# GpSimd rounds the context of the cross-attention, and ScalarE writes one more mask

## What is computed

```python
K = split(jnp.einsum('bsd,ed->bse', key, wk))
V = split(jnp.einsum('bsd,ed->bse', value, wv))
scores = jnp.einsum('bhqd,bhkd->bhqk', Q, K) / np.sqrt(hd)
scores = jnp.where(mask[:, None, :, :] == 1, jnp.float32(-1000000000.0), scores)
attn = jax.nn.softmax(scores, axis=-1)
out = jnp.einsum('bhqk,bhkd->bhqd', attn, V)
```

## Time and profile before

| | |
|---|---|
| median of three runs | 1336.21 us (1335.66 to 1337.94) |
| the profiled execution | 1324.22 us, of which the span takes 1322.4 |
| mean granted TensorE clock | 0.967 of full speed |
| busy: TensorE matmuls, VectorE, ScalarE, GpSimd | 1221.1, 899.4, 761.3, 498.6 us |
| the steps of the attention | about 498 to 1054 us of the span |

### The profile page before, as it was taken

How to read it: one execution, slowest core, us unless ns; L and a number is a source line. 1 busy time by engine, 2 the same in 40 slices (tenths; PEclk the granted TensorE clock), 3 DMA queues, 4 the chain that set the end, 5 groups by cost and what they waited for, 6 DMA issues and landing times.

```text
span 1322.4 us, 34415 instructions
## 1 busy us (share of the span) xinstructions
PE 1221.1 (92%) x10866; PEld 1107.4 (84%) x10866; DVE 899.4 (68%) x2932; ACT 761.3 (58%) x1780; POOL 498.6 (38%) x709
## 2 busy tenths in 40 slices
PE   5899999999997788999999999999999988999984
PEld 4788889899897677889999999899998777888884
DVE  4684664856746456788788888888887575555548
ACT  3444344333442226788888888888888854555530
POOL 2332240422412323344444444444444541333335
PEclk9999999999998898999999999999999898999997
DMA  8499700000000235566666665556665143333358
GB/s 206 106 232 239 176 0 0 0 0 0 0 0 23 57 76 140 141 142 153 153 149 154 152 151 148 145 147 150 152 157 148 52 136 93 101 106 98 106 141 249
DMA packets 131263, 151.39 MB, mean 114 GB/s; under 512 B 41107, under 2 KB 111108, under 8 KB 131156
## 3 DMA queue, kind: packets, MB, share of 16 engines
q1 hardware_dynamic: 124436, 134.55, 42.1%
q0 software_dynamic: 6160, 15.69, 3.5%
q10 hardware_dynamic: 576, 0.07, 0.0%
HBM read 79.27 MB, written 45.82 MB: 95 GB/s over the span
## 4 chain that ended last, share of the span: by engine, by line
PE 50%; DVE 4%; issue 2%; ACT 2%; DMA 2%; POOL 1%; SPq 1%; DVEq 0%; POOLq 0%; ACTq 0%
PE psum L875 9%; PE psum L1124 7%; PE psum L1161 6%; PE psum L1147 6%; PE psum L1296 6%; PE psum L1316 3%; PE psum L1093 2%; PE psum L1142 2%; PE psum L1189 2%; PE psum L1175 1%; DVE x_res L2333 1%; PE psum L1208 1%; PE psum L1287 1%; PE psum L1304 1%; DVE x_res L2327 1%
## 5 line engine op out<-in xcount | busy, mean ns | idle before, releaser
L2196 DVE CUSTOM_DVE_ANT_0 junk<-psum,biasq 112x375 f32<-112x375 f32 x512 | 267.5, 542 | 93.2 <-issue 60.1
L1653 ACT ACTIVATE pr<-psum 125x448 f32<-125x448 f32 x384 | 204.1, 540 | 37.5 <-PE psum L1147 35.8
L1147 PE MATMUL psum<-qst,kst 97*125 97x224 f32 x768 | 194.4, 319 | 5.4 <-ACT psum L1662 5.2
L1124 PE MATMUL psum<-kst,qst 96*112 96x376 f32 x512 | 170.1, 357 | 3.6 <-DVE smax L2196 3.2
L1147 PEld LDWEIGHTS psum<-qst,kst 97*125 97x125 f32 x768 | 139.2, 192 | 19.6 <-ACT psum L1662 13.2
L1662 ACT ACTIVATE psum<-flagk 125x448 f32<-125x448 bf16 x256 | 140.4, 549 | 6.7
L717 POOL TENSOR_TENSOR rs<-rs,neg_half 112x1 f32<-112x1 f32 x32 | 18.2, 569 | 244.3 <-DVE rs L2109 244.3
L841 POOL DMA_INDIRECT routed_y<-yb,yrow x61 | 58.7, 962 | 123.9 <-ACT yb L1843 119.7
L1124 PEld LDWEIGHTS psum<-kst,qst 96*112 96x112 f32 x512 | 89.8, 180 | 15.0 <-issue 5.8
L1161 PE MATMUL psum<-pr,vaug 125*32 125x112 f32 x3072 | 96.3, 267 | 0.0
L759 POOL DMA_INDIRECT routed_h<-h,slot x64 | 74.7, 1166 | 32.3 <-POOL h L748 14.8
(11 more groups left out here) (320 smaller groups left out, 3529.5 us busy)
## 6 DMA issues: line engine op xcount, KB each, us to landing
kst<-khi SPq DMA_DIRECT2D x64, 376.0 KB, 4.9
routed_h<-in_route_pad SPq DMA_DIRECT2D x6, 3640.0 KB
kst<-klo SPq DMA_DIRECT2D x32, 376.0 KB, 6.1
ctxT<-in_ctxT SPq DMA_DIRECT2D x32, 375.0 KB, 3.5
hblk<-routed_h SPq DMA_DIRECT2D x61, 130.0 KB, 2.1
qst<-qhi SPq DMA_DIRECT2D x128, 56.0 KB, 2.5
stage<-in_e SPq DMA_DIRECT2D x21, 256.0 KB, 3.1
maskq<-in_mask SPq DMA_DIRECT2D x32, 164.1 KB
```

Of the source, the lines that this page charges most:

```text
L1124: pe.matmul(bank[max_bank(n, par, hd)][0:T, 0:S2E], head(qst[par][0:ROWS], hd), pair(kst[par][0:ROWS], hd // 2), start=True, stop=True).th ...
L1147: mm = pe.matmul(bank[q % 2][0:KP, cols(i, 2 * T)], pair(kst[par], n)[:, cols(q // HPB, KP)], both(qst[par], n), start=False, stop=True, s ...
L1653: nc.scalar.activation(pr[q % PROBS][:].rearrange("k i q -> k (i q)"), bank[q % 2][0:KP, 0:GT], ACT.Exp, scale=1.0 / HD ** 0.5).then_inc(s ...
L2196: nc.vector.tensor_tensor_reduce(out=junk[:, hd % 2, :], in0=bank[max_bank(n, par, hd)][0:T, 0:S2], in1=biasq[:, par, :], scale=1.0, scala ...
```

## The change

ScalarE no longer rounds the context from row 3 on. GpSimd does it with a `tensor_copy`, for row b + 3 in step b, right behind its second power and ahead of `decide`. Slot 11 joins the table of written slots: ScalarE writes its mask behind the exponential of slot 9, and TensorE's mask matmul of slot 11 falls away.

```diff
-WRITTEN = (2, 3, 4, 6, 7, 8, 9, 10)
+WRITTEN = (2, 3, 4, 6, 7, 8, 9, 10, 11)
@@ GpSimd
+            def high_context(t, par):
+                f = t * RB + par
+                wait_apart(pool, s2["ctx_in"], 16 * (f + 1))
+                wait_apart(pool, s2["v_ps"], f)
+                nc.gpsimd.tensor_copy(chi[:, :, 0:S2], ctxT[:]).then_inc(s2["c_hi"], 1)
@@ GpSimd, step
                 if power:
                     rsqrt(*ahead(t, par, 3))
+                if context:
+                    high_context(*ahead(t, par, 3))
                 if early >= 2:
                     decide(*ahead(t, par, -2))
@@ ScalarE, step
-                    if q == 0 and following >= 2 and not first:
-                        high_context(*far)
...
-                    if q + 2 in WRITTEN and q < 8:
+                    if q + 2 in WRITTEN and q != 8:
                         write_mask(t, par, q + 2)
```

More of the change, by code:

```diff
@@ L769, in low_shared, with step @@
                 nc.gpsimd.tensor_tensor(h3lo[g % 2][:], raw, h3hi[g % 2][:].bitcast(F32), op=ALU.subtract).then_inc(s["ht_lo"], 1)
-            def step(t, par, masks=True, power=True):
+            def step(t, par, masks=True, power=True, context=True):
                 early = t * RB + par if isinstance(t, int) else 2 * RB
@@ L814, in _ @@
             for par in range(RB):
-                step(ROUNDS, par, power=ROUNDS * RB + par + 3 < B)
-            step(ROUNDS + 1, 0, masks=False, power=False)
+                step(ROUNDS, par, power=ROUNDS * RB + par + 3 < B, context=ROUNDS * RB + par + 3 < B)
+            step(ROUNDS + 1, 0, masks=False, power=False, context=False)
             scatter(*ahead(ROUNDS + 1, 1, -4))
```

## The result

Beside the same runs of the kernel before, the change takes 1344.3 us (median of 6) where that one takes 1336.3: ratio 1.0056, 95% interval 1.0043 to 1.0070. That is slower by about 8.0 us, inside the range given and 5.8 us above the forecast.

The account below looks back on a forecast made before the run. TensorE and ScalarE were taken to run in step, so the removed matmul becomes a wait. Terms +1.2, +0.8 and +0.3 sum to +2.3 us on the median 1336.2: 1338.5 us, range 1333 to 1345.5.

Parts of the forecast that it names:

- the same: Whole kernel: time change within 0.2% (2.7 us), what a measurement can tell from no change; chance 0.51.
- term 2: Slot 11 on TensorE: ScalarE's mask comes too late, next load 0.04 us later in 29 steps, +1.2 us.
- term 6: Between steps 1 and 2: cast ahead of GpSimd's three subtractions delays VectorE's scaling L2114 and TensorE by 0.80 us, +0.8 us.
- Terms 1 and 2: Slot 11: TensorE's mask matmul of 0.18 us a step goes, replaced by a wait for ScalarE's mask; +1.2 us.
- Matmul won: Rival, slot 11: the mask matmul's 0.18 us is saved in every step, 5.4 us in all, 1332 us; chance 0.13.
- Terms 3 to 5: Cast leaves ScalarE, takes 0.80 us on GpSimd, blocks VectorE's scaling; TensorE's transposes still met with 0.27 us spare; cost 0.
- Term 7: GpSimd's `decide`, scatter and masks move 0.8 us back; their readers come a step or more later: 0.
- Term 8: Step 30, no keys or values to make: ScalarE's mask delays slot 11's exponential, +0.3 us.
- The base: Starting time: profiled execution 1324.2 us, 12 us below the median; same difference put on the median, 1336.2 to 1338.5 us.

Follow-up runs that it names:

- e12: The change, unedited, third comparison against the kernel before: 1325.7 us beside 1322.6, ratio 1.0026 (1.0017 to 1.0034).
- e11: The kernel before, unedited, profiled a third time: 1322.2 us beside 1322.6, ratio 1.0000 (0.9990 to 1.0011).
- e7: Kernel before plus only GpSimd's cast, with the scatter moved behind the masks: 1321.8 us beside 1321.7, ratio 0.9998 (0.9986 to 1.0011).
- e9: The change, unedited, compared again with the kernel before: 1341.2 us beside 1336.5, ratio 1.0036 (1.0023 to 1.0049).
- e3: The whole change plus GpSimd's scatter moved behind the masks, against the kernel before: 1332.5 us beside 1335.2, ratio 0.9975 (0.9963 to 0.9986).
- e10: The change with the scatter behind the masks, e3 unedited, against the kernel before: 1332.5 us beside 1336.5, ratio 0.9972 (0.9959 to 0.9984).
- e5: Kernel before with only GpSimd's scatter moved behind the masks: 1323.1 us beside 1321.7, ratio 1.0009 (1.0000 to 1.0019).

## Why the prediction was right and wrong

The direction of the sum and the range held; the forecast of "the same" (0.51) did not. That 1344.3 us lies in the range is in part luck: its upper end stood for a cast of up to 1.3 us, and the cast took 0.80. The forecast itself reached to 1341 us. On the lower level, where its rows came from, the sum of +2.3 us met +3.4, with two errors against each other: term 2 was 2.5 us short, term 6 1.5 us too high.

- **Terms 1 and 2** (the mask matmul traded for a wait; 96 mask matmuls are left of 128): right in mechanism and to 0.01 us at slot 11's load. The step that failed is "with 0.22 us for the two scores the next load comes at 814.89": true in one step of three, 0.18 us short in the others, where four sequencer entries that used to be worked off ahead come only after the wait. 0.04 us a step was 0.16, +1.2 us was +3.7 (e12 against e11). "Matmul won" (0.13) never showed.
- **Terms 3 to 5** (cast off ScalarE, 0.80 us on GpSimd, L2120 blocked until 0.15 us after it, transposes met): right, 800 ns, 1.41 us, and no cost in e7. The cast starts at 826.36 and the next instruction at 827.14, so the spacing of starts gives 0.78 us; the 1.02 us that the Trainium skill's rule of spacings (Perfetto Trace Analysis, section "GPSIMD Engine Instruction") gave from the small cast was too long, because 0.22 of that cast's 0.60 us was the next instruction's wait for it.
- **Term 6**: wrong in sign. I let the cast lengthen the block of L2114; it came in between, after L2120 was through, and the block moved to a scaling that no transpose waits for. The first five steps together came out at about -0.7 us, where the term had +0.8; what else moved in them is not taken apart.
- **Term 7** (choice of experts and scatter 0.8 us later, "0"): right on the lower level. On the upper it is the step that failed: I asked only who reads the results of these instructions, not what their issue does to others. The change loses 8.0 and 4.7 us there and 3.4 on the lower level; 1.3 to 4.6 us more than its own cost go with the held signals, and moving the scatter, nothing else, takes 8.7 us away beside e9, and by the two ratios about 10.8 between e3 and the change's first comparison. Shown is that the scatter's place matters; how the cast and the mask divide the rest is not.
- **Term 8**: +0.07 us in the last three steps, where the term had +0.3.
- **The base.** "I put the same difference on the median" joined a profile of the lower level to times of the upper. The 12 us between them was the one sign ahead of the result that the step in the profile was not the step that was timed, and I used it as an offset instead of asking what it was made of.

## What to carry to other kernels

A wait put in the place of an instruction costs more than the time waited when the sequencer has register and wait work behind it: here each entry up to the next load took some 0.1 us, four of them cost 0.18 us a step and two cost nothing. When work on the engine that issues indirect DMAs is shifted, ask where those issues land against the signals on the critical path, and not only who reads their data. And when a profiled execution stands 12 us off the median, a sum of 2 us made on it needs that gap explained first.

## What the runs showed of the hardware

On the upper level the two issues of the scatter go with stretches in which semaphore updates of TensorE, VectorE and ScalarE are held back; TensorE's then come 34 to 43 ns apart. Between 560 and 1030 us of e10 TensorE has 57 recorded ends of semaphore-raising matmuls between 1.0 and 1.3 us after an indirect DMA's start, and 2 updates; between 1.4 and 1.7 us it has 54 ends and 93 updates. In the first of these stretches VectorE has 39 ends and 6 updates, ScalarE 25 and 4. In e5, the late scatter on the lower level, TensorE has 63 ends and 65 updates there, VectorE 29 and 29, ScalarE 37 and 36. The issues themselves take the same on both levels (1.04 and 1.05 us in the mean for the change).

And the holding of VectorE by GpSimd (the Trainium skill, SBUF — State Buffer, section "Who interferes with whom", has the one that issues first keep the port pair) again can't be told from who starts first in the trace: L2120, 0.44 to 0.46 us ahead of the cast, lost 1.0 us in 27 steps and nothing in one, between steps 1 and 2, where it was 0.435 us ahead. All seven profiles with the cast have this one exception in the same place, and in all it is the step with the smallest distance, 0.435 to 0.438 us against 0.439 to 0.460. A scaling that is not held takes 0.41 us and would be over before the cast's recorded start, so the recorded starts can't be taken for the order in which the two got hold of what they share. What decides it is open.
